# Value products of a pair's first quarter joined to the second quarter's, on the tensor engine of one Trainium2 core

## The reference

```python
q = apply_rotary(q, cos, sin) * DHEAD ** (-0.5)
k = apply_rotary(k, cos, sin)
kt = jnp.einsum('bhnd,hde->bhne', k, W_bilinear)
sim = jnp.einsum('bhid,bhjd->bhij', q, kt)
attn = jax.nn.softmax(sim, axis=-1)
out = jnp.einsum('bhij,bhjd->bhid', attn, v)
```

## Time and profile before

| | |
|---|---|
| median of 3 runs | 3471.37 us (3470.07 to 3475.37) |
| profiled execution | 3466.45 us |
| its span, first to last instruction | 3464.6 us |
| PE, DVE, ACT, POOL busy | 98%, 76%, 67%, 75% |
| mean granted clock of PE | 0.991 of full speed |
| matmul records | 21410 |

### The profile page before, as it was taken

One profiled execution on the slowest core, in us unless ns is written; L12 is line 12 of the kernel. 1 busy time (PEld: TensorE's weight loads), 2 busy tenths in 40 slices (PEclk: granted clock), 3 DMA queues, 4 the chain that ended last, 5 costly groups with the idle time before them and its releaser, 6 DMA issues. The chain is left out here.

```text
span 3464.6 us, 71914 instructions
## 1 busy us (share of the span) xinstructions
PE 3398.6 (98%) x21410; PEld 2200.6 (64%) x21410; DVE 2636.0 (76%) x4493; ACT 2313.3 (67%) x4412; POOL 2606.4 (75%) x1279
## 2 busy tenths in 40 slices
PE   6999999999999999999999999999999998899999
PEld 4655555555555555555555556566666664799998
DVE  6777777777777767777777777777777777899998
ACT  2666677666667766666766676677766666566665
POOL 2888888888889878888888888898888886122222
PEclk7999999999999999999999999999999999999999
DMA  5222323333323223332333333223322223333332
GB/s 197 83 88 95 119 94 102 102 123 102 102 92 117 98 98 102 118 102 96 99 123 102 102 102 119 96 94 100 118 90 93 75 74 113 101 100 100 102 105 69
DMA packets 255089, 355.75 MB, mean 103 GB/s; under 512 B 40220, under 2 KB 163484, under 8 KB 250268
## 3 DMA queue, kind: packets, MB, share of 16 engines
q1 hardware_dynamic: 245532, 343.29, 30.5%
q10 hardware_dynamic: 9216, 8.39, 0.7%
HBM read 219.49 MB, written 62.12 MB: 81 GB/s over the span
## 5 line engine op out<-in xcount | busy, mean ns | idle before, releaser
L463 POOL TENSOR_TENSOR prob_sum<-prob_sum,prob 128x1024 f32<-128x1024 f32 x762 | 1860.7, 2442 | 363.5 <-ACT prob L542 312.8
L542 ACT ACTIVATE prob<-scores 128x512 f32<-128x512 f32 x2048 | 1073.8, 600 | 525.8 <-PE scores L828 514.0
L752 DVE TENSOR_REDUCE row_max<-max_scores 128x1 f32<-128x512 f32 x1536 | 987.6, 684 | 428.0 <-PE max_scores L870 410.2
L1033 PE MATMUL attn_out<-prob,v 128*64 128x512 f32 x4096 | 934.3, 598 | 0.0
L819 PE MATMUL scores<-q_hi,k_hi 64*128 64x512 f32 x2048 | 785.5, 416 | 8.5 <-ACT prob L542 4.6
L824 PE MATMUL scores<-q_hi,k_lo 64*128 64x512 f32 x2048 | 755.5, 395 | 0.0
L828 PE MATMUL scores<-q_lo,k_hi 64*128 64x512 f32 x2048 | 751.8, 393 | 0.0
L1033 PEld LDWEIGHTS attn_out<-prob,v 128*64 128x64 f32 x4096 | 277.4, 137 | 565.3 <-issue 541.6
L870 PE MATMUL max_scores<-k_hi,q_hi 64*128 64x512 f32 x1536 | 578.9, 430 | 8.7 <-DVE row_max L752 5.5
L513 ACT ACTIVATE scores<-neg_max_seeds 128x512 f32<-128x512 f32 x1024 | 552.7, 598 | 42.7 <-DMA neg_max_seeds<-neg_max_halves 42.2
L819 PEld LDWEIGHTS scores<-q_hi,k_hi 64*128 64x128 f32 x2048 | 376.5, 185 | 284.0 <-issue 126.0
(11 more groups left out here) (148 smaller groups left out, 4771.9 us busy)
## 6 DMA issues: line engine op xcount, KB each, us to landing
rows<-rows SPq DMA_DIRECT2D x512, 128.0 KB, 2.0
neg_max_seeds<-neg_max_halves SPq DMA_DIRECT2D x128, 512.0 KB, 3.9
w_group<-w_parts SPq DMA_DIRECT2D x30, 1536.0 KB, 8.4
attn_normalised<-z_stage SPq DMA_DIRECT2D x128, 256.0 KB, 2.1
v<-attn_normalised SPq DMA_DIRECT2D x64, 512.0 KB, 4.1
sum_inverted_rows<-sums_inverted SPq DMA_DIRECT2D x126, 256.0 KB, 4.1
x_turned_parts<-x_tile_parts SPq DMA_DIRECT2D x49, 256.0 KB, 2.8
xt_batch<-x_turned_parts SPq DMA_DIRECT2D x7, 1792.0 KB, 10.3
```

Of the source, the lines that this page charges most:

```text
L463: nc.gpsimd.tensor_tensor(sums_of(k, half), a, prob[:, n % RING, :, :], ALU.add).then_inc(added, 1)
L542: nc.scalar.activation(prob[:, n % RING, e, :], S[e][n % 2][:, :], ACT.Exp).then_inc(exped[e], 1)
L752: nc.vector.reduce_max(mx[1 - u][:, e, n // 2, n % 2:n % 2 + 1], bank_of(e, jj)[:, :], axis=AX.X)\
L1033: nc.tensor.matmul(O[rows(e), :], V[k // 2 % 2][:, j, col:col + DH], prob[:, n % RING, e, :], start=j == 0, stop=j == 7).then_inc(pv_made[ ...
```

## The change

Four things change. The value products of quarter 0 are no longer issued behind the work of quarter 0, but behind the second burst, in one run with quarter 1's. The maxima of quarter 1 take the banks O, M, X[1] in turn and no longer X[0], X[1], M. `norm_z` moves on VectorE from the end of quarter 0 to behind the maxima of quarter 1. On SyncE the seeds' rows and the columns of the sums go ahead of the stored output. The waits follow from that: the first maximum of quarter 1 waits for the copy out of O, the second for the rotation of the queries' first half, the third for the copied sums, the others for the read of the maximum three places before; the value products wait for the read of the seventh maximum.

```diff
-        def bank_of(e, jj):
+        def bank_of(e, jj, q):
 
-            return (X[0], X[1], M)[MAX_ORDER.index((e, jj)) % 3]
+            return ((O, M, X[1]) if q == 1 else (X[0], X[1], M))[MAX_ORDER.index((e, jj)) % 3]
...
+                if attn:
+                    max_seeds(t - 1, 1)
+                if k >= 1:
+                    sum_columns(t - 1)
                 if k >= 2:
                     for h in two:
                         store_z(k - 2, t - 2, h)
-                if k >= 1:
-                    sum_columns(t - 1)
-                if attn:
-                    max_seeds(t - 1, 1)
...
-                    if q == 0 and k >= 2:
-                        norm_z(k - 2, t - 2)
                     if q == 2 and k == -2:
                         constants()
                     if q == 1 and has_tile(k):
                         offset(t)
+                    if q == 1 and k >= 2:
+                        norm_z(k - 2, t - 2)
...
+                elif q == 1:
+                    if i == 0:
+                        wait(pe, z_copied, 2 * t)
+                    elif i == 1:
+                        if proj:
+                            wait(pe, sin_made[Q], 2 * pp + 1)
+                        else:
+                            wait(pe, x_red[1], 16 * (t + 1) + 2)
+                    elif k >= 1:
+                        wait(pe, l_copied, t)
+                    elif attn:
+                        wait(pe, nm_hi, 2 * t + 2)
+                    else:
+                        wait(pe, x_red[1], 16 * (t + 1) + 4)
+                elif q == 2:
+                    if i == 0 and proj:
+                        wait(pe, sin_made[Q], 2 * pp + 2)
+                    else:
+                        wait(pe, x_red[1], 16 * (t + 1) + (3, 6, 8)[i])
...
-                        for jj in range(4):
-                            n = 4 * q + jj
+                        if q == 1 and prep:
+                            wait(pe, x_red[1], 16 * (t + 1) + 7)
+                        for n in ((), range(8), range(8, 12), range(12, 16))[q]:
                             j = n % 8
```

More of the change, by code:

```diff
@@ L751, in span @@
                             wait(dve, x_made[e], 16 * (t + 1) + n + 1)
-                            nc.vector.reduce_max(mx[1 - u][:, e, n // 2, n % 2:n % 2 + 1], bank_of(e, jj)[:, :], axis=AX.X)\
+                            nc.vector.reduce_max(mx[1 - u][:, e, n // 2, n % 2:n % 2 + 1], bank_of(e, jj, q)[:, :], axis=AX.X)\
                                 .then_inc(x_red[e], 1)
@@ L848, in max_score @@
                     wait(pe, lo_made[K], 2 * (t + 1) + 2)
-                elif i == 1:
[L850 to L865, removed]
+                elif q == 0:
+                    if i == 1:
+                        wait(pe, x_red[1], 16 * (t + 1))
+                elif q == 1:
[17 more added lines that the diff above has]
+                        wait(pe, x_red[1], 16 * (t + 1) + (3, 6, 8)[i])
+                elif i == 1:
+                    wait(pe, nm_hi, 2 * (t + 1) + 1)
+                    if has_tile(k):
+                        wait(pe, x_lo, 2 * (t + 3))
+                elif proj:
@@ L866, in max_score @@
                     wait(pe, v_copied, 2 * pp + (2 if i == 0 else 1))
-                elif q:
+                else:
                     wait(pe, x_red[1], 16 * (t + 1) + 4 * q - (1 if i == 0 else 2))
                 tile, part = n // 2, n % 2
-                nc.tensor.matmul(bank_of(e, jj)[:, :], QH[v][rows(e), tile * P:(tile + 1) * P], KH[v][rows(e), cols(part)],
+                nc.tensor.matmul(bank_of(e, jj, q)[:, :], QH[v][rows(e), tile * P:(tile + 1) * P], KH[v][rows(e), cols(part)],
```

## The result

The changed kernel takes 3596.4 us (median of 4 runs, 3593.6 to 3598.3) against 3471.8 us: ratio 1.0357, 95% interval 1.0339 to 1.0375. It is 125 us slower; 99 were forecast, and 3596 lies inside the stated range of 3530 to 3630 and inside the forecast's own of 3540 to 3605.

What follows compares the result with a forecast made beforehand. TensorE, busy 98%, was taken to bound the kernel with a fixed string of work. 69 + 38 - 10 - 10 + 12 = +99 us; 3466.45 + 99 + 4.9 = 3570 us, range 3530 to 3630.

Steps and rivals of the forecast that it cites:

- Part 1: Second burst, moved up: its fourth maximum waits for VectorE to end the queries' rotation, mean 1.13 us in 61 pairs, +69 us.
- Part 2: Merged product run: waits for O until the seventh maximum is read, 0.61 us in each of 62 pairs, +38 us.
- Part 3: Value products: joining two runs saves 0.15 us of entering and leaving, 64 times, -10 us.
- Part 4: Third burst: earlier seeds' DMA saves 0.16 us in 62 pairs, -10 us; the moved inverse products cost nothing.
- Part 5: TensorE's clock: long waits drop it to half in 5 pairs, 2.5 us each, +12 us.
- Rival A: Second burst: rotation ends before the first maximum is there, only the product wait stands; +18 us, 3489 us, chance 0.06.
- B: TensorE's clock falls in most pairs, 155 us in place of 12; 3713 us, chance 0.10.
- C: Faster: earlier seeds and shorter SyncE queue bring the rotation forward, both TensorE waits vanish; 3451 us, chance 0.04.
- D: Product run not joined in effect, each matmul waiting for its own exponential at ScalarE's pace; no change, 3471 us, chance 0.02.

Runs made afterwards that it cites:

- the narrow instruction: Changed kernel with VectorE's low part of the queries' second half (L732) made for 8 columns in place of 512: 3562.3 us.
- the narrow adds: GpSimd's first three adds of a pair made for 8 columns of each 512: 3523.8 us in the changed kernel, 3462.4 in the kernel before.

## Why the prediction was right

The mechanism was right: TensorE waits for VectorE at the two places named, and the third that shows, the second maximum's wait for M, lies within the first one (it was put at under 0.2 us and is 0.5). The sizes were not all right, and the errors partly cancel.

**Part 1, the rotation (69 us): right in kind, too small.** The burst's fourth maximum waits 3.01 - 1.28 = 1.73 us in the mean, 61 x 1.73 = 106 us. The step that failed is the start of the last L742, which I took from the old trace as it stood, 1.07 us behind the start of the product run (that is the median of the 61 pairs; their mean is 1.10). It is 1.68, because L732 ahead of it grew by 0.84 us in the mean. A part of that is taken back, since L742 now waits for the swapped rows 3 times, 1.3 us in all, where it did 24 times, 18.1 us.

Why did it grow? In the kernel before GpSimd ran behind the exponentials: ahead of the first add of a pair it waited for one in 1 of 61 pairs. In the slower pair it has caught up and waits there in all 61 (0.76 us in the pair shown; the first adds of the halves, 127 of them, were idle for it for 30.7 us in all before and for 128.7 after). With that the adds stand at a fixed place in the pair, and L732 meets the third of them with 1.92 us left in the mean, where before it met an add with 1.04 left, and twice the scatter. It does not take the join: in the two runs that moved the inverse products and joined nothing, whose pairs are longer too, L732 takes 2.41 and 2.26 us in the mean. That the adds hold L732 up is shown by the narrow instruction and by the narrow adds; that the catching up fixes their phase is read from these traces, not tried by itself. The Trainium skill ("SBUF — State Buffer", "Who interferes with whom") says that a VectorE instruction with two SBUF inputs contends with a GpSimd one that reads SBUF, that the port pair which they share is an exclusive lock, and that the order of issue decides who blocks; the 8-column row agrees, it ends 0.02 us behind the add. L732 and L619 are of that kind; the rotation and the maxima, which read one operand or none from SBUF, keep their 0.68 us throughout (0.67 to 0.70 in both kernels).

**Part 2, the products' wait (38 us): right, with less effect.** The products start 0.05 us after the end of the seventh read (1551.59 against 1551.54), 0.6 us later than the burst alone would allow. But the burst, held up once, runs its rest faster: seventh behind fourth maximum 2.45 us, where the earlier trace rows have 2.72. So the two waits together lengthen the burst by 2.19 us, not 2.34, and part 2 adds about 28 us where 38 were forecast.

**Part 3, the join (10 us): about half.** The joined run takes 7.09 us behind a wait, against 3.58 + 3.58; 7.02 where it needs none. Saved 0.07 to 0.15 us a pair.

**Part 4, the seeds (10 us): right.** The third burst is at 4.50 us. SyncE's order alone gave 13 us. The statement in the same part that the inverse products cost nothing held only by the cover of the joined run: they take 4.17 us in their new place, more than the 2.55 us that I counted on, and without the join that costs 198 us.

**Part 5, the clock (12 us): too high, it is nothing.** Two falls of 3.4 us each stand against the one of 6.8 us that the kernel before has in the same part, at 1249.7: the time at half clock is the same. What the step had wrong is the length of one stop. The waits of 1.9 to 2.3 us in one piece, for which I had let 5 pairs fall, did not come; they are cut into shorter ones.

Together: +37 for part 1, -10 for part 2, +5 for part 3 and -12 for the clock turn 99 into 119, against 125 measured; the burst near the end of the attention part brings 5 more. That part 1 came out half as large again and the total only a quarter larger is luck: parts 2 and 5 were too high and made up for it. Rival A fell with the rotation's rows, B with the clock, C with the rotation that does not wait for SyncE in most pairs (the waits for the swapped rows were 18.1 us in all, over 24 pairs), D with the burst's length.

## What to carry to other kernels

Before work that covers another engine is moved, write down what it covers and until when that engine is busy: here 0.15 us of switching was bought with 3.6 us of cover. Bank orders move such a wait about (3562, 3596 and 3671 us for three of them) but don't remove it. And an instruction's length in the old trace is not its own where it holds a wait for another engine's instruction: L732's 1.59 us were 0.9 of waiting; a change of the period can shift the two against each other in every pair.

## What the runs showed of the hardware that was not expected

- A VectorE subtraction with both inputs in SBUF takes 0.68 us alone and up to 2.7 beside GpSimd's adds of 2.40 us; on 8 columns it takes 0.16 us alone and 1.94 beside an add, and ends 0.02 us behind it.
- Waiting costs more in one piece: one stop of about 1.9 us a pair (121 us in the run) came with the clock at 1.2 GHz in 45 stretches, three stops a pair that make more together (166 us) in 10, and three of about half a microsecond or less in two.
